# Layers 2 and 3 of a four-layer graph network: the aggregation with the turned attention in two row halves of 64, into two PSUM banks

## The reference, cut to what matters

```python
Wh     = einsum('bnd,de->bne', x, W)                 # 512 -> 512
logits = (Wh @ a_src)[:, :, None] + (Wh @ a_dst)[:, None, :]
logits = where(logits >= 0, logits, 0.2 * logits)
logits = where(adj == 0, -inf, logits)
attn   = softmax(logits, axis=-1)                    # per graph 64 x 64
out    = einsum('bnm,bmd->bnd', attn, Wh)
x      = layernorm(x + out)
```

## Time and profile before

| what | value |
| --- | --- |
| median of 3 runs | 3140.3 us (3139.85 to 3141.08) |
| the profiled execution, its own time | 3139.89 us |
| its span in the trace | 3138.2 us |
| TensorE (PE) busy | 3074.8 us, 98% |
| weight loads (PEld) busy | 2691.9 us, 86% |
| VectorE (DVE) busy | 2297.8 us, 73% |
| GpSimd (POOL) busy | 2061.9 us, 66% |
| ScalarE (ACT) busy | 1776.1 us, 57% |

### The profile page before, as it was taken

The page is one execution under the profiler, slowest core; times in us unless marked ns, Lnnn a source line. Parts: engine busy times, 40 slices in busy tenths (PEclk is TensorE's granted clock), DMA queues, the critical chain, the costliest instruction groups (busy, mean ns, idle before and its releaser), DMA issues.

```text
span 3138.2 us, 64986 instructions
## 1 busy us (share of the span) xinstructions
PE 3074.8 (98%) x19593; PEld 2691.9 (86%) x19593; DVE 2297.8 (73%) x4825; ACT 1776.1 (57%) x4325; POOL 2061.9 (66%) x2773
## 2 busy tenths in 40 slices
PE   8999989999999999999999999999899999999997
PEld 6888878889988888898889889888688888888885
DVE  6777656777777776777777777765788888888886
ACT  3333335555555555555555555543577777777775
POOL 5666635666666666666666656641688888888886
PEclk9999999999999999999999999999899999999999
DMA  6555411111111111111111111114332333223220
GB/s 198 178 190 177 151 46 40 41 50 50 47 53 40 53 40 55 45 47 53 47 47 40 60 40 47 53 41 155 91 97 82 100 94 97 86 91 100 90 74 28
DMA packets 181766, 244.46 MB, mean 78 GB/s; under 512 B 15808, under 2 KB 81344, under 8 KB 181696
## 3 DMA queue, kind: packets, MB, share of 16 engines
q1 hardware_dynamic: 169920, 218.46, 21.5%
q10 hardware_dynamic: 9216, 16.78, 1.4%
q0 software_dynamic: 2560, 8.39, 0.8%
HBM read 159.68 MB, written 83.89 MB: 78 GB/s over the span
## 4 chain that ended last, share of the span: by engine, by line
PE 76%; issue 5%; POOL 3%; ACT 1%; DVE 1%; DMA 0%; SPq 0%; POOLq 0%; ACTq 0%; DVEq 0%
PE wop L2020 23%; PE hp L2006 20%; PE wop L47 9%; PE hp L2171 5%; PE hp L47 5%; PE agg L1989 4%; PE shared L2028 2%; PE agg L2131 2%; PE shared L2131 2%; POOL w_first L1223 1%; PE shared L248 1%; PE hp L2158 1%; POOL g_terms L1291 1%; PE smallp L200 1%; POOL cols L389 0%
## 5 line engine op out<-in xcount | busy, mean ns | idle before, releaser
L1223 POOL TENSOR_TENSOR w_first<-xd,v_row 128x512 f32<-128x512 f32 x480 | 682.5, 1435 | 346.1 <-DMA xd<-x_scratch 315.3
L2006 PE MATMUL hp<-yT_hi,big_hi 128*128 128x256 f32 x2048 | 595.1, 291 | 0.0
L2006 PE MATMUL hp<-yT_hi,big_lo 128*128 128x256 f32 x2048 | 580.1, 283 | 0.0
L2006 PE MATMUL hp<-yT_lo,big_hi 128*128 128x256 f32 x2048 | 579.8, 283 | 0.0
L2020 PE MATMUL wop<-big_hi,hT_hi 128*128 128x512 f32 x1024 | 424.8, 415 | 0.4 <-ACT v_row L1404 0.4
L2020 PE MATMUL wop<-big_hi,hT_lo 128*128 128x512 f32 x1024 | 402.1, 393 | 0.0
L2020 PE MATMUL wop<-big_lo,hT_hi 128*128 128x512 f32 x1024 | 400.5, 391 | 0.0
L2006 PEld LDWEIGHTS hp<-yT_hi,big_hi 128*128 128x128 f32 x2048 | 392.8, 192 | 7.5 <-DVE yT_lo L1698 0.7
L2006 PEld LDWEIGHTS hp<-yT_lo,big_hi 128*128 128x128 f32 x2048 | 392.7, 192 | 3.0 <-issue 0.2
L2006 PEld LDWEIGHTS hp<-yT_hi,big_lo 128*128 128x128 f32 x2048 | 392.7, 192 | 0.0
L1291 POOL TENSOR_TENSOR g_terms<-x,g_v_row 128x512 f32<-128x512 f32 x256 | 368.1, 1458 | 35.3 <-ACT x L1557 33.5
(11 more groups left out here) (218 smaller groups left out, 8115.2 us busy)
## 6 DMA issues: line engine op xcount, KB each, us to landing
x0f<-in_x_turned SPq DMA_DIRECT2D x64, 256.0 KB, 2.7
xt<-in_x SPq DMA_DIRECT2D x64, 256.0 KB, 2.9
x_scratch<-w_first ACTq DMA_DIRECT2D x64, 256.0 KB, 2.2
xa<-x_scratch SPq DMA_DIRECT2D x64, 256.0 KB, 2.7
att_hi_scratch<-att_hi SPq DMA_DIRECT2D x64, 256.0 KB, 2.0
att_lo_scratch<-who SPq DMA_DIRECT2D x64, 256.0 KB, 2.0
att_scratch<-attT SPq DMA_DIRECT2D x64, 256.0 KB, 2.0
att_hi<-att_hi_scratch SPq DMA_DIRECT2D x64, 256.0 KB, 3.7
```

Of the source, the lines that this page charges most:

```text
L1223: nc.gpsimd.tensor_tensor(terms[:, k % TR, :], xd[:], v_row[:, k, :], ALU.mult).then_inc(terms_ready, 1)
L2006: ins = nc.tensor.matmul(hp[half][:, s * 2 * P:(s + 1) * 2 * P], a, b, start=c == 0 and i == 0, stop=c == KC - 1 and i == 2)
```

## The change

Layers 2 and 3 take layer 1's form. `turned` becomes 64 columns wide: the two blocks stand on their own 64 partitions, and the zero blocks, their memsets and the semaphore go. `aggregate3` issues 8 matmuls in place of 4, each with 64 rows of x as the stationary operand and 64 moving columns, the graphs in turn. Graph b's results go to bank b of `agg`; layer 2 has the lower half of both banks, layer 3 the upper half. So layer 2's small products move to `shared`. Since both layers now use both banks, an aggregation waits until VectorE has read the other layer's last one. `agg_hi3` and `agg_lo` read two banks and write in an order that puts the graphs side by side as before. The output attention of the last two tiles (`last_sums`, `last_exp`, `out_elu`) goes the same way, into `agg`. For tile T - 1 its exponential, ELU and cast move from the end of step 2 to earlier places in it, and layer 2's first aggregation waits for the ELU.

```diff
@@ SlotAttention
-        self.turned = piece(6 * NODES, P)
+        self.turned = piece(6 * NODES, NODES)
...
-    def pool_zero(self, nc):
-        nc.gpsimd.memset(self.turned, 0.0).then_inc(self.zeroed, 1)
...
     def act_turned(self, nc, act, t):
         act.wait_ge(self.turned_done, t + 1)
-        if isinstance(t, int) and t == 0:
-            act.wait_ge(self.zeroed, 1)
         for g in range(2):
             r = slice(g * NODES, (g + 1) * NODES)
-            nc.scalar.copy(self.turned[r, :, r], self.turned_psum[r, :, r]).then_inc(self.turned_ready, 1)
+            nc.scalar.copy(self.turned[r, :, :], self.turned_psum[r, :, r]).then_inc(self.turned_ready, 1)
@@ banks
-            agg_2, agg_3 = (bank.rearrange("p (c n) -> p c n", c=KC) for bank in (agg[:, 0, :], shared[:]))
-            small_2, small_3 = agg[:, 1, :], smallp[:]
+            agg_2, agg_3 = (agg[:, :, q * KC * NODES:(q + 1) * KC * NODES].rearrange("p g (c n) -> p g c n", c=KC)
+                            for q in range(2))
+            small_2, small_3 = shared[:], smallp[:]
@@ ScalarE
+                def last_exp(s):
+                    act.wait_ge(uo_done, s + 1)
+                    act.wait_ge(att_stored, 16 * s)
+                    nc.scalar.activation(turned_att(), agg_2, ACT.Exp).then_inc(exo_ready, 1)
...
-                    nc.scalar.copy(g.aggS[0][:], g.agg[:]).then_inc(g.agg_hi_ready, 1)
+                    nc.scalar.copy(by_graph(g.aggS[0][:]), g.agg).then_inc(g.agg_hi_ready, 1)
...
                         normalise3(n_1, n - 1, z1[:], x2[(r - 1) % R][:], x2_ready)
+                    if isinstance(n, int) and n == 2:
+                        last_exp(T - 1)
+                        split_att(T - 1, PAIRS)
                     if live(n, 2):
                         turned3(g2, n - 2)
...
                         dot3(g2, n - 1, 1)
-                    if isinstance(n, int) and n == 2:
-                        out_exp(T - 1)
-                        split_att(T - 1, PAIRS)
@@ VectorE
                     if live(n, 2):
                         after_exp(g2, n - 2)
+                    if isinstance(n, int) and n == 2:
+                        out_elu(T - 1)
...
-                    if isinstance(n, int) and n == 2:
-                        out_elu(T - 1)
@@ TensorE
+                def last_sums(s, j):
+                    pe.wait_ge(ao_.turned_ready, 2 * s + 2)
+                    for c in range(KC):
+                        for b in range(2):
+                            own = slice(b * NODES, (b + 1) * NODES)
+                            ins = nc.tensor.matmul(agg_2[:, b, c, :], who[j][own, c * P:(c + 1) * P],
+                                                   ao_.turned[own, 0, own], start=True, stop=True)
+                    ins.then_inc(uo_done, 1)
+
                 def aggregate3(g, t, x):
                     pe.wait_ge(g.att.turned_ready, 2 * t + 2)
-                    ge(pe, g.agg_lo_ready, t)
                     for c in range(KC):
-                        ins = nc.tensor.matmul(g.agg[:, c, :], x[:, c * P:(c + 1) * P], g.att.turned[:, 0, :],
-                                               start=True, stop=True)
+                        for b in range(2):
+                            own = slice(b * NODES, (b + 1) * NODES)
+                            ins = nc.tensor.matmul(g.agg[:, b, c, :], x[own, c * P:(c + 1) * P],
+                                                   g.att.turned[own, 0, :], start=True, stop=True)
                     ins.then_inc(g.agg_done, 1)
...
                     if live(n, 5):
+                        pe.wait_ge(g2.agg_lo_ready, capped(n - 2, T))
+                        ge(pe, g3.agg_lo_ready, n - 5)
                         aggregate3(g3, n - 5, x3[(r - 5) % R])
...
                     if live(n, 2):
+                        if isinstance(n, int) and n == 2:
+                            pe.wait_ge(att_ready, T)
+                        if live(n, 5):
+                            pe.wait_ge(g3.agg_lo_ready, n - 4)
+                        ge(pe, g2.agg_lo_ready, n - 2)
                         aggregate3(g2, n - 2, x2[(r - 2) % R])
```

More of the change, by code:

```diff
@@ L321, in __init__ @@
         self.prob = slot[:, 4 * NODES:6 * NODES].rearrange("p (h g n) -> p h g n", h=1, g=2)
-        self.turned = piece(6 * NODES, P)
+        self.turned = piece(6 * NODES, NODES)
         self.f, self.peak, self.total, self.inv = cols[:, 0:2], cols[:, 8:9], cols[:, 16:17], cols[:, 24:25]
-        self.zeroed, self.f_ready, self.diag_ready = sem("zeroed"), sem("f_ready"), sem("diag_ready")
+        self.f_ready, self.diag_ready = sem("f_ready"), sem("diag_ready")
         self.scores_done, self.summed, self.leaky = sem("scores_done"), sem("summed"), sem("leaky")
@@ L1010, in gnn_stack_kernel @@
             g3 = Gat("g3", 3 * KC, agg_3, small_3, wop[1], g3_own, 256, g3_rows, g3_terms, g3_agg, g3_z)
-            g2.wide, g3.wide = wop, (wop[1], shared)
+            g2.wide, g3.wide = wop, (wop[1], smallp)
             weights = (w1, w2, W2, W3)
@@ L1033, in run, with by_graph, turned_att @@
                     step(p)
+            def by_graph(x):
+                return x.rearrange("p c (g n) -> p g c n", g=2)
+            def turned_att():
+                return attT[:].rearrange("p (c g n) -> p g c n", c=KC, g=2)
             def pair(p):
@@ L1330, in _ @@
                 split_att(2 * m - 1, 1)
-                g2.att.pool_zero(nc)
                 pool.wait_ge(h_done, 8 * PAIRS)
                 pool.wait_ge(at.turned_done, T)
-                g3.att.pool_zero(nc)
                 ao_.pool_diag(nc, pool, 2 * m, i64)
@@ L1667, in _ @@
                 ao_.act_exp(nc, act, 2 * m + 1)
-                out_exp(2 * m)
+                last_exp(2 * m)
                 keep_att(1)
@@ L1739, in out_elu @@
                     dve.wait_ge(nego_ready, s + 1)
+                    if isinstance(s, int) and s >= T - 2:
+                        nc.vector.tensor_tensor(turned_att(), agg_2, turned_att(), ALU.max).then_inc(att_ready, 1)
+                        return
                     nc.vector.tensor_tensor(attT[:], shared[:], attT[:], ALU.max).then_inc(att_ready, 1)
@@ L1843, in agg_lo @@
                     dve.wait_ge(g.agg_hi_ready, t + 1)
-                    nc.vector.tensor_tensor(g.aggS[1][:], g.agg[:], g.aggS[0][:].bitcast(F32), ALU.subtract
-                                            ).then_inc(g.agg_lo_ready, 1)
+                    nc.vector.tensor_tensor(by_graph(g.aggS[1][:]), g.agg, by_graph(g.aggS[0][:].bitcast(F32)),
+                                            ALU.subtract).then_inc(g.agg_lo_ready, 1)
                 def scores(g, t):
@@ L2216, in step3 @@
                         pe.wait_ge(att_ready, T - 1)
-                        out_sums(T - 1, 1)
+                        last_sums(T - 1, 1)
                     if isinstance(n, int) and n == 3:
-                        pe.wait_ge(att_ready, T)
                         spread_rows(g3)
@@ L2246, in _ @@
                 first_half(2, 2)
-                out_sums(2 * m, 0)
+                pe.wait_ge(y_lo_ready, 8 * PAIRS)
+                last_sums(2 * m, 0)
                 pe.wait_ge(ao_.turned_ready, 2 * (2 * m + 1))
```

## The result

The changed kernel takes 3187.68 us (median of 4 runs, 3186.05 to 3189.17), the kernel before on the same chip 3140.07 (4 runs, 3139.69 to 3141.08). The ratio is 1.0151 [1.0133, 1.0169]: 47.6 us slower; the interval of the ratio is 41.8 to 53.1 us. The forecast was 41.7 us slower (3182, range 3174 to 3191), so sign and size hold, and 5.9 us are missing. The profiled execution took 3187.77 us, its span is 3186.1.

What follows compares the result with a forecast made beforehand. TensorE, full from 2260 to 3060 us, was taken to bound the kernel. Full stage 36.3, step 2's order 2.4, rest of passage 1.0 and end 2.0 make 41.7 us more: 3182 us, range 3174 to 3191.

Steps and rivals of the forecast that it cites:

- the full stage: 2260 to 3060 us, TensorE always busy: 56.8 steps, each 0.64 us longer (14.09 to 14.73), +36.3 us.
- the order in step 2: Passage, 2150 to 2260 us: tile T - 1's exponential and cast ahead of L352's copies delay TensorE's first layer-2 aggregation, +2.4 us.
- the rest of the passage: 2150 to 2260 us: four aggregations and two `last_sums`, 1.9 us in all, of which half was taken, +1.0 us.
- the end: 3060 to 3138 us: eleven aggregations, 3.5 us at most; as TensorE has gaps there, +2.0 us.
- The pace: TensorE's aggregations: weight loads 0.11 us apart pace the records, so 16 half records cost as much as 8 full ones.
- the switch: Each aggregation, going to row halves and back: 0.40 and 0.34 less 0.05, so +0.35 us layer 2, +0.29 layer 3.
- The waits for the other layer's `agg_lo`, the casts, the copies: Each step: new TensorE waits, casts and subtractions from two banks, and block copies, all forecast to add 0.
- The records' duration: Next profile's TensorE records of the aggregations' half matmuls: 217 ns forecast.
- Columns as the pace: Rival for the aggregations: columns pace the pairs, 0.06 us each; about 3142 us, no change; 5%.
- A hidden switch: Rival for the aggregations: columns pace the pairs and short matmuls hide the stall; faster, about 3094 us; 2%.
- One by one: Rival for the aggregations: halves don't run side by side, 0.89 us more each, about +100 us on top, 3283; 2%.
- A wait for `agg_lo`: Rival in the full stage: late casts make `project3` wait, up to 0.3 us a step more, 3199 us; 5%.

Runs made afterwards that it cites:

- the run with 64 columns: Kernel before, each full-array aggregation matmul cut in two of 64 columns, all 128 rows and zero blocks kept: 3254.57 us, ratio 1.036.
- the pair of runs with one small matmul: Kernel before plus one 64-column matmul a step ahead of the feed-forward's second product: with 64 rows 3175.89 us, with 128 rows 3156.89 us.

## Why the prediction held, point by point

Term by term between the two spans: the full stage came out 1.8 us below its forecast, the order in step 2 0.8 above, the rest of the passage 3.0 above, the end 3.9 above, and 0.3 lies ahead of tile 2. These make the 6.2 us by which 47.9 exceeds 41.7. The main term carries the result; the small terms erred mostly one way.

**The full stage: right.** Forecast 14.73 us a step and +36.3; measured 14.72 at one step, +34.5 over 56. The pace (a load sets it, a pair of halves loads in the time of one) is shown by the half loads of 0.97 us and by the run with 64 columns; the switch (forecast 0.40 and 0.34 from layer 1's rows, less 0.05) by the pair of runs with one small matmul, 0.34. That tenths of a step survive the sum is because TensorE never waits in this stage: 824.10 of 824.10 us busy. Two readings from the timeline make 0.63 a step, the stage 0.616: over 56 steps the mean is 14.10 before (the one step read for the forecast took 14.09) and 14.72 after. Of the 1.8 us by which the stage fell short, 56 steps in place of 56.8 make 0.5, and the rest is those hundredths.

**The waits for the other layer's `agg_lo`, the casts, the copies: right at 0.** The groups of the casts and the subtractions of the changed kernel, from two banks, answer to the earlier trace rows:

```profile
L1549 ACT CAST g_agg_hi<-agg 128x512 fp32r<-128x512 f32 x128 | 75.5, 590 | 64.4 <-PE agg L2151 64.3
...
L1854 DVE TENSOR_TENSOR g_agg_lo<-agg,g_agg_hi 128x512 fp32r<-128x512 f32 x128 | 87.9, 686 | 30.1 <-ACT g_agg_hi L1549 30.1
```

590 ns against 587, and 686 against 691. TensorE has no wait for another engine in the full stage.

**VectorE's work in a step: not foreseen, without effect.** From 2280 to 3040 us another subtraction, the feed-forward part's `h1T_lo`, takes twice as long as before. First the kernel before, then the changed one:

```profile
L1888 DVE TENSOR_TENSOR h1T_lo<-h,h1T_hi 128x512 fp32r<-128x512 f32 x54 | 37.6, 696 | 54.3 <-ACT h1T_hi L1586 54.3
```

```profile
L1898 DVE TENSOR_TENSOR h1T_lo<-h,h1T_hi 128x512 fp32r<-128x512 f32 x52 | 71.4, 1373 | 66.2 <-ACT h1T_hi L1593 66.2
```

The longer step shifts it against GpSimd's product (L1295). In 38 of the 52 steps the product starts first, and the subtraction lasts 1.56 to 1.68 us. In the other 14 the subtraction starts first and lasts 0.69 us, and then the product takes 1.75 to 1.81 us instead of 1.27. The time doesn't show it, since TensorE waits for nothing here.

**The records' duration: wrong, without effect.** I expected 217 ns for a half record of 64 columns. The line's own view:

```profile
L2151 PE MATMUL agg<-g_own,x x2048: 271/272/475, 2220.0 to 3173.8; 64*128 64x64 f32 x187
```

271 ns at the least, exactly as layer 1's with 128 columns. The 54 ns that I took off came out nevertheless, in the group: 16 records last 1.11 us here and 1.16 in the earlier trace rows.

**Step 2's order: right mechanism, too small by 0.8 us.** Forecast +2.4, measured +3.2 (undone 3.3, alone 3.1). The delay runs from the exponential's start to the cast's end, and ScalarE's timeline of the changed kernel has it:

```profile
2216.32 0.59 ACT L1395 ACTIVATE attT<-agg 128x512 f32<-128x512 f32 x1
2218.92 0.62 ACT L1406 CAST att_hi<-attT 128x512 fp32r<-128x512 f32 x1 [2.01 <-DVE attT L1748]
2219.44 0.43 ACT L347 COPY g_own<-shared 64x64 f32<-64x64 f32 x2
```

It is 2219.54 - 2216.32 = 3.22 us where the earlier trace rows gave 2.42. The 0.8 us are VectorE's:

```profile
2216.94 1.22 DVE L1744 TENSOR_SCALAR attT<-attT 128x512 f32<-128x512 f32 x1 [2.38 <-ACT attT L1395]
```

It took 1.22 us here, and 0.43 both in before and in the run with the order undone. The new place in the step puts it beside GpSimd's two products, here by their own line's view:

```profile
L1295 POOL TENSOR_TENSOR g_terms<-x,g_v_row x2: 1257/1353/1449, 2216.6 to 2217.8; 128x512 f32<-128x512 f32 x2
```

The first of them ends at about 2217.9, VectorE's instruction at 2218.16. In the kernel with that order alone VectorE's instruction takes 1.22 us too, again during GpSimd's first product; in the two kernels with the late order GpSimd is idle just then and it takes 0.43. The Trainium skill (SBUF — State Buffer, section Who interferes with whom) has VectorE's `tensor_scalar` in its fast mode and a GpSimd instruction exclude each other for a whole instruction. The four profiles agree with that, and so do the 38 and 14 steps above for a subtraction, where the one that starts second is the one that takes longer; an experiment that moves GpSimd's product alone was not made. The step that failed: I took the durations of the three instructions from their old place, and did not look at who would run beside them at the new one.

TensorE behind it: the first aggregation of layer 2 waited 4.64 us for the copy, against 1.28 in the earlier trace rows:

```profile
2220.02 1.97 PE L2151 MATMUL agg<-g_own,x 64*128 64x64 f32 x16 [4.64 <-ACT g_own L347]
```

**The rest of the passage: too small.** Forecast +1.0 for six aggregations, measured +4.0 from tile 3 to tile 6. 1.9 of that appears with the order alone, where there are no halves, and there it is the clock's: from layer 2's first aggregation to the feed-forward product behind the projections the same instructions take 8.90 us (2223.71 to 2232.61) against 7.02 in before (2216.52 to 2223.54), and their matmuls of 512 columns start 0.43 us apart where before has 0.23. Yet it doesn't go away when the order is undone (55.1 again), and the changed kernel itself gave 53.4 in its second profile. Wherever the stretch is long, the clock is at 0.84, where before has 0.89. In before the last 11.10 us ahead of the full stage (2258.40 to 2269.50) ran at the full clock; in after the corresponding 15.10 us (2261.90 to 2277.00) had a mean of 0.82, with TensorE busy throughout in both. The step that failed is the same as at the end, below: six aggregations were priced at the full clock, and the clock of the stretch was put at nothing. How much of the 4.0 is the clock and how much the aggregations, these runs don't separate.

**The end: too small, and the clock is why.** Forecast +2.0 for eleven aggregations, measured +5.9. The run with step 2's order undone has the same program at the end, and its end is 81.2 us, +2.1. That this meets the 2.0 is in part luck: its mean clock is 0.93 where before has 0.96. The first 50 us of the end are alike in both. Then, in windows of 10 us, the changed kernel:

```profile
3151.10:3161.10 10.00, 9.84 (x42) 7.46 (x40) 4.12 (x14) 3.88 (x9) 4.22 (x10) 0.66 0.07 27
3161.10:3171.10 10.00, 6.30 (x29) 5.00 (x30) 3.35 (x11) 5.10 (x13) 4.25 (x9) 0.69 0.07 27
```

and the one with the order undone:

```profile
3148.50:3158.50 10.00, 8.73 (x43) 6.40 (x41) 5.57 (x17) 4.73 (x14) 4.76 (x11) 0.83 0.07 28
3158.50:3168.50 10.00, 6.76 (x41) 5.34 (x43) 3.25 (x10) 4.70 (x12) 3.72 (x7) 0.83 0.07 26
```

In both, the clock is still at 1.00 in the window ahead of these, with TensorE busy 8.6 of 10 us. Then it is at its lower level (1.2 GHz) for a part of each window: 0.66 and 0.69 mean some two thirds of the time at half clock, 0.83 one third. Over the whole end that is 0.12 x 2 x 85.0 = 20 us at half clock against 0.07 x 2 x 81.2 = 11. Nine us more at half clock go with 3.8 us more of time, and the timeline shows that the one makes the other. The same two matmuls behind layer 2's aggregation, in the changed kernel and in the one with the order undone:

```profile
3155.49 0.63 PE L47 MATMUL wop<-w_lo,g_agg_hi 128*128 128x512 f32 x1
3155.91 0.63 PE L47 MATMUL wop<-w_hi,g_agg_lo 128*128 128x512 f32 x1
```

```profile
3152.59 0.40 PE L47 MATMUL wop<-w_lo,g_agg_hi 128*128 128x512 f32 x1
3152.82 0.40 PE L47 MATMUL wop<-w_hi,g_agg_lo 128*128 128x512 f32 x1
```

They start 0.42 us apart at the half clock and 0.23 at the full one. At three places the changed kernel is at half clock where the other is at full: 3154.89 to 3158.29 us (3.40 us against 1.95 for the same instructions), 3169.64 to 3171.75 (2.11 against 1.17) and 3175.43 to 3178.57 (3.14 against 1.72). The differences, 1.45, 0.94 and 1.42, make the 3.8 us. The failed step: I priced the end by instructions at the full clock. Why the same instructions got the lower clock for longer in one kernel than in the other, no run here settles.

**The rivals.** Columns as the pace: fell. A hidden switch: fell, at 0.34 us each. One by one: not in the changed kernel; with the loops exchanged it comes up in part. A wait for `agg_lo`: none in the full stage. No version tried beats the kernel before.

## What to carry to other kernels

Before halving a matmul's rows, find what paces its records: compare the spacing of its weight loads with that of a matmul with fewer columns. If the load paces them, as in this kernel's float32 matmuls of 128 columns or fewer, two halves do no more than one full record, and each visit to the half-array form costs 0.34 us on top; halves pay when the columns pace the full record and the saving is larger than the switch (256 columns: 0.43 us won for 4 matmuls). When a step is moved, price its instructions by what runs on the other engines at the new place, and price stretches in which TensorE has gaps at the clock that they get.

## What the runs showed of the hardware that was not expected

- A half record of 64 columns is recorded at 271 ns, as one of 128 columns, while a full-array record of 64 columns goes down to 217 ns.
- Halves of one graph in a row don't pair up, but the last loads of one half and the first of the other do: 1.47 us for 16 loads, between 0.97 and 1.84.
- VectorE's `tensor_scalar` of 128x512 took 1.22 us beside a GpSimd product and 0.43 without one; its subtraction `h1T_lo` took 1.56 to 1.68 us when GpSimd's product had started first and 0.69 otherwise.
- TensorE's clock at the kernel's end was 0.88 in two profiles of the changed kernel and 0.93 in one whose end has the same instructions.
